# Eight token groups, a recurrence of 512 steps beside them: the second group's projections move into the third group's experts, and the recurrence serves the groups at other steps

## The reference, cut to what matters

```
k = l2norm(silu(x @ Wk)); v = silu(x @ Wv); q = silu(x @ Wq)
a = k * -sigmoid(x @ Wg);  f = sigmoid(x @ Wf1 @ Wf2)
for t in range(512):
    S = S + a[t] (x) (k[t] . S)
    S = f[t] * S
    S = S + a[t] (x) (k[t] . S) + k[t] (x) v[t]
    o[t] = q[t] . S
out = layernorm(o_placed * sigmoid(x @ Wo1 @ Wo2)) * ln_w @ Wout
```

## Time and profile before

| | us |
|---|---|
| median of 3 runs | 5178.53 |
| lowest and highest of them | 5151.21, 5182.2 |
| the profiled execution, its own time | 5154.96 |
| its span, first to last instruction | 5153.2 |
| PE, DVE, ACT, POOL busy in it | 4309.6, 3271.6, 2603.5, 1814.6 |
| mean granted clock of PE | 0.893 of full |

### The profile page before, as it was taken

The page is one execution under the profiler, slowest core; times in us unless marked ns, Lnnn a source line. Parts: engine busy times, 40 slices in busy tenths (PEclk is TensorE's granted clock), DMA queues, the critical chain, the costliest instruction groups (busy, mean ns, idle before and its releaser), DMA issues.

```text
span 5153.2 us, 114063 instructions
## 1 busy us (share of the span) xinstructions
PE 4309.6 (84%) x43126; PEld 2583.4 (50%) x43126; DVE 3271.6 (63%) x14115; ACT 2603.5 (51%) x5100; POOL 1814.6 (35%) x3734
## 2 busy tenths in 40 slices
PE   4689999999999999975699999778750079999999
PEld 4545555555555555545544446545520034446777
DVE  3187777777777777733177741699999867762111
ACT  1346777777777777751344544444430034553333
POOL 3255666666666666663132210000100023220000
PEclk9879999999999999986788989888865568998999
DMA  4500000000000000004401000010010000000000
GB/s 125 145 10 2 3 12 2 7 8 2 12 2 2 12 2 7 2 1 114 115 8 38 1 1 13 13 26 16 16 34 0 12 1 1 1 1 3 5 5 7
DMA packets 125108, 101.75 MB, mean 20 GB/s; under 512 B 22384, under 2 KB 103568, under 8 KB 124560
## 3 DMA queue, kind: packets, MB, share of 16 engines
q1 hardware_dynamic: 119952, 85.00, 6.0%
q0 software_dynamic: 4608, 9.45, 0.8%
HBM read 74.56 MB, written 19.86 MB: 18 GB/s over the span
## 4 chain that ended last, share of the span: by engine, by line
PE 58%; DVE 22%; POOL 10%; issue 4%; ACT 4%; DMA 1%; SPq 0%; POOLq 0%; DVEq 0%; ACTq 0%; PEldq 0%
PE ps L1746 6%; PE ps L1738 6%; PE ps L1357 5%; PE ps L1302 5%; PE ps L1502 4%; PE ps L1514 4%; PE ps L1278 4%; PE ps L1317 3%; PE ps L1288 3%; PE ps L1231 3%; PE ps L1543 2%; POOL arena L990 2%; POOL arena L995 2%; PE ps L1187 2%; DVE arena L2824 2%
## 5 line engine op out<-in xcount | busy, mean ns | idle before, releaser
L2294 DVE CUSTOM_DVE_ANT_0 arena<-ps,mask_win 128x256 f32<-128x256 f32 (+1 forms) x3072 | 1006.0, 386 | 156.6 <-PE ps L1302 155.7
L1910 ACT ACTIVATE arena<-ps 128x512 f32<-128x512 f32 (+1 forms) x1536 | 752.7, 544 | 490.0 <-PE ps L1317 487.5
L1317 PE MATMUL ps<-arena 32*64 32x384 f32 (+2 forms) x6144 | 703.1, 475 | 8.4 <-DVE arena L2294 7.1
L1302 PE MATMUL ps<-arena 32*64 32x192 f32 (+2 forms) x12288 | 683.6, 322 | 15.9 <-DVE arena L2294 15.4
L1746 PEld LDWEIGHTS ps<-w,arena 128*128 128x128 f32 x4096 | 544.4, 195 | 265.9 <-issue 223.0
L2174 ACT ACTIVATE arena<-ps,eb 128x512 f32<-128x512 f32 x512 | 351.7, 688 | 548.8 <-PE ps L1738 548.7
L2467 DVE CUSTOM_DVE_ANT_0 arena<-ps,mask_cau 128x512 f32<-128x512 f32 (+3 forms) x1024 | 446.6, 487 | 251.3 <-PE ps L1502 248.8
L2027 ACT ACTIVATE arena<-ps 128x512 f32<-128x512 f32 (+2 forms) x768 | 362.9, 526 | 456.2 <-PE ps L1514 456.1
L990 POOL TENSOR_SCALAR_AFFINE_SELECT arena<-arena 128x1024 f32<-128x1024 f32 x384 | 419.9, 1094 | 491.4 <-ACT arena L1910 486.1
L1746 PE MATMUL ps<-w,arena 128*128 128x128 f32 x4096 | 551.0, 278 | 26.6 <-ACT arena L2174 26.6
L1738 PE MATMUL ps<-arena,w 128*128 128x512 f32 x1024 | 534.5, 605 | 0.4
(11 more groups left out here) (348 smaller groups left out, 7572.2 us busy)
## 6 DMA issues: line engine op xcount, KB each, us to landing
w<-in_L_w_dram SPq DMA_DIRECT2D x160, 256.0 KB, 3.5
ys<-arena SPq DMA_DIRECT2D x10, 512.0 KB, 4.5
hs<-arena SPq DMA_DIRECT2D x16, 256.0 KB, 2.3
w<-in_L_w_dram SPq DMA_DIRECT2D x1, 2048.0 KB
scr_k<-arena SPq DMA_DIRECT2D x8, 256.0 KB, 2.3
scr_v<-arena SPq DMA_DIRECT2D x8, 256.0 KB, 2.9
scr_f<-arena SPq DMA_DIRECT2D x8, 256.0 KB, 3.2
arena<-scr_k SPq DMA_DIRECT2D x8, 256.0 KB, 3.5
```

The costliest lines, as they stand in the source:

```text
L1302: m = pe.matmul(ps[64 * h:64 * h + 64, bank, s.at(v) + lo:s.at(v) + hi], Q[p][r][rows, v, q0:q0 + 64], K[p][r][rows, s.k0 + lo:s.k0 + hi], ...
L1317: m = pe.matmul(out[64 * h:64 * h + 64, :, lo:hi], K[p][r][rows, t.k0 + lo:t.k0 + lo + 64], Q[p][r][rows, 0:2, t.q0 + lo:t.q0 + hi], start ...
L1910: act.activation(PTs[m % L.SLOTS][:, k * w:(k + 1) * w], bank[:, 0:w], exp, scale=-1.0)\
L2294: x = dve.tensor_tensor_reduce(out=seen, in0=bank[:, s.at(v):s.at(v) + s.kw], in1=mask, scale=1.0, scalar=NO_SCORE, op0=ALU.add, op1=ALU.m ...
```

## The change

Projections: every group but the last is now projected inside the experts of the group behind it. `normed` stands at pass 11 and `projected`/`project` at pass 15 as before for even groups, now for all, except group 1 in group 2: passes 4 and 7. The experts run through from group to group. `by_time(0)` stands at pass 13 of group 2, `by_time(1)` and `by_time(2)` at pass 27 of groups 4 and 6, `by_time(3)` at the end. Recurrence: the services stand at steps 4, 28, 64, 94 and 114 of a chunk. The first chunk's root is made by DVE itself instead of POOL. `kt_ready` counts each of the three copies, so that the squares wait for the keys' copy alone and `prepare` for all three.

```diff
+    def normed_at(self, g):
+        return 4 if g == 1 else 11
+    def projected_at(self, g):
+        return 7 if g == 1 else 15
+    def by_time_at(self, c):
+        return 13 if c == 0 else 27
...
                 if c:
-                    sp.wait_ge(R.kt_ready, c)
+                    sp.wait_ge(R.kt_ready, 3 * c)
...
-                    pool.wait_ge(R.n2_ready, c + 1)
-                    newton(pool, chain, RN, N2, T1)
-                    pool.sem_inc(R.rn_ready, 1)
+                    if c:
+                        pool.wait_ge(R.n2_ready, c)
+                        newton(pool, chain, RN, N2, T1)
+                        pool.sem_inc(R.rn_ready, 1)
...
-                        if s == 15 and beside:
+                        if use == 0 and g and s == R.projected_at(g - 1):
                             project(g - 1)
                         if s:
                             down(g, *order[s - 1])
-                        elif g and (use or beside):
+                        elif g:
                             down(g - 1, *order[-1])
...
-                    if beside:
-                        down(g, *order[-1])
-                        if S.scaled(use, g):
-                            add(g, EXPERTS - 1)
-                        project(g)
-                if use:
-                    down(S.GROUPS - 1, *order[-1])
+                g = S.GROUPS - 1
+                down(g, *order[-1])
+                if use == 0:
+                    add(g, EXPERTS - 1)
+                    project(g)
...
                     for dst, src in ((KT, KD), (FT[c % 2], FD), (VT[c % 2], VD)):
-                        m = act.activation(dst, src.rearrange("p k t -> p t k"), copy)
-                    m.then_inc(R.kt_ready, 1)
+                        act.activation(dst, src.rearrange("p k t -> p t k"), copy).then_inc(R.kt_ready, 1)
...
-                            if (e, c) == (2, 3) and beside:
+                            if use == 0 and g and at == R.normed_at(g - 1):
                                 normed(g - 1)
-                            if (e, c) == (3, 3) and beside:
+                            if use == 0 and g and at == R.projected_at(g - 1):
                                 projected(g - 1)
-                            if (e, c) == (1, 3) and use == 0 and g in (4, 6):
+                            if use == 0 and g in (2, 4, 6) and at == R.by_time_at(g // 2 - 1):
                                 by_time(g // 2 - 1)
...
                 def lengths(c):
-                    dve.wait_ge(R.kt_ready, c + 1)
+                    dve.wait_ge(R.kt_ready, 3 * c + 1)
...
-                    dve.tensor_scalar(N2, N2, 1e-24, None, ALU.max).then_inc(R.n2_ready, 1)
+                    m = dve.tensor_scalar(N2, N2, 1e-24, None, ALU.max)
+                    if c:
+                        m.then_inc(R.n2_ready, 1)
+                        return
+                    chain.link(m)
+                    newton(dve, chain, RN, N2, T1)
...
-                    dve.wait_ge(R.rn_ready, c + 1)
+                    if c:
+                        dve.wait_ge(R.rn_ready, c)
+                    dve.wait_ge(R.kt_ready, 3 * c + 3)
...
-                    if at == 28:
+                    if at == 4:
                         add_bank(0, g)
                         stats_of(g)
-                    if at == 54:
+                    if at == 28:
                         silu(g)
-                    if at == 86:
+                    if at == 64:
                         add_bank(0, g + 1)
                         stats_of(g + 1)
-                    if at == 108:
+                    if at == 94:
                         silu(g + 1)
-                    if at == 123:
+                    if at == 114:
                         lengths(c + 1)
```

More of the change, by code:

```diff
@@ L1787, in dense @@
                 for g in range(S.GROUPS):
-                    beside = use == 0 and g % 2
                     for s, (e, c) in enumerate(order):
@@ L2169, in dense @@
                 for g in range(S.GROUPS):
-                    beside = use == 0 and g % 2
                     for e in range(EXPERTS):
                         for c in range(CHUNKS):
+                            at = CHUNKS * e + c
                             act.wait_ge(S.up_done, S.result(use, g, e) * CHUNKS + c + 1)
@@ L2187, in dense @@
                                 scale(g, e - 1)
-                            if (e, c) == (0, 3) and beside and S.scaled(use, g - 1):
+                            if (e, c) == (0, 3) and g and S.scaled(use, g - 1):
                                 scale(g - 1, EXPERTS - 1)
-                    if beside:
-                        if S.scaled(use, g):
-                            scale(g, EXPERTS - 1)
-                        normed(g)
-                        projected(g)
-                        if g in (1, S.GROUPS - 1):
-                            by_time(g // 2)
+                if use == 0:
+                    g = S.GROUPS - 1
+                    scale(g, EXPERTS - 1)
+                    normed(g)
+                    projected(g)
+                    by_time(g // 2)
             attention(cau, 0, 0)
```

4 lines of the change are left out of this document (2 added, 2 removed).

## The result

The changed kernel takes 5183.41 us (median of 20 runs, 5168.01 to 5204.09); the kernel before, run beside it, 5166.34 (20 runs, 5147.94 to 5189.39). The ratio is 1.003, with a 95% interval of 1.0017 to 1.0044: slower by 17 us in the medians, 9 to 23 by the interval, which is inside the 1% that the prediction takes for no change. The prediction said 5182 and no change. Its class is right, and that the number is so close is luck: it stood on a median of three runs, 5178.53, that lies 12 us above the median of twenty, and the change cost 17 and not 3.4.

What follows compares the result with a forecast made beforehand. DVE's recurrence was taken to bound the stretch, through its start and its waits. The terms sum to +3.4 us: 5158 from the profiled 5154.96, 5182 from the median 5178.53, where the forecast was put; range 5139 to 5202.

Steps and rivals of the forecast that it cites:

- The start: Ahead of chunk 0: `prepare(0)` starts 1.9 us earlier, at 3264.9, with ACT last and Newton on DVE taking 4.0.
- Step 4: In chunk 0, DVE waits 7.6 us for group 2's bank instead of 2.94: 4.7 lost; bounds 2 and 14.
- 5.0 more: PE behind gelu 13 of group 2: `by_time(0)`, a scaling and the next gelu, partly hidden, delay the bank by 5.0 us.
- slower rival: Services come too soon for PE, which restarts at low clock after standing: +20 us, so 5199; chance 0.17.
- The rest of chunk 0: Waits of 0.7 us at steps 28 and 64, none at 94 and 114; the 1.85 before `prepare(1)` goes: +1.5 - 1.85.
- Chunk 1: Waits of 1.6 us for group 5's bank and 3.3 for keys, against 2.1 and 1.86 before: +0.9 in all.
- the same sum: Change over the whole kernel, added from start and chunks: -1.9 + 4.7 + 1.5 - 1.85 + 0.9 = +3.4 us.
- chunk 2: Last part counted: group 7's bank is early and the waits for q stay, so nothing is added.
- PE's gap: Rival: PE's 41 us gap between groups 1 and 2 is on the path, so the end comes at 5137; chance 0.04.
- Waits did come in place of the old ones: Against the rival that old waits go and none comes in the recurrence: -11.6 us, so 5167; chance 0.17.

## Why the class was right and the sum was not

**The start** held. The prediction had the copies 40.8 us behind group 1's last gelu and found them at 40.3; Newton 4.0, measured 4.05; `prepare(0)` 1.9 earlier, measured 2.2. That ACT and not the DMA would be last held too. (The signs that the prediction gives as times of a trace, as `prepare(0)` between 3260 and 3270, have to be read 24.9 us later in the trace after, by what the untouched part ahead took longer there: 3289.48 less 24.89 is 3264.6.)

**Step 4** had the right mechanism and a term too small: 7.6 us forecast, 10.1 measured, within the bounds of 2 and 14. DVE's arrival was forecast at 86.1 us of the stretch and came at 85.7. The bank was forecast at 93.7 and came at 95.8. The step that failed is "5.0 more" for the time that `by_time(0)` holds PE: from the end of gelu 13 to the bank 52.9 us were forecast and 55.5 came, 2.6 more, and gelu 13 itself ended 0.4 early. PE's timeline and two windows (busy PE first, the granted clock third from the end) show what was left out:

```profile
3282.51 1.02 PE L1750 MATMUL ps<-arena,w 128*128 128x512 f32 x2
3288.39 2.07 PE L1758 MATMUL ps<-w,arena 128*128 128x128 f32 x8 [4.85 <-ACT arena L2182]
```

```profile
3288.39:3293.37 4.98, 4.98 (x12) 3.21 (x13) 4.73 (x9) 0.52 (x1) 0.00 (x0) 0.50 0.00 0
3293.37:3336.22 42.85, 42.72 (x233) 29.63 (x232) 31.63 (x42) 23.19 (x47) 0.00 (x0) 1.00 0.00 1
```

PE stood 4.85 us as counted, and then worked 4.98 us at the 1.2 GHz level, eight downs in 2.07 instead of 1.05. At half the clock that is some 2.5 us lost, nearly all of the 2.6; the 47.9 us of before, to which the 5.0 were added, ran at a clock of 1.00 throughout:

```profile
3287.47:3335.39 47.92, 47.79 (x258) 32.94 (x257) 42.62 (x100) 25.81 (x53) 0.00 (x0) 1.00 0.00 1
```

The prediction had this in its slower rival and in its upper bound, but not in the forecast.

**The rest of chunk 0** held nearly to the row: bank to bank 77.1 forecast, 77.13 measured; 0.7 and 0.7 against 0.69 and 0.86. **Chunk 1** too: 1.6 and 3.3 against 1.23 and 2.96, and PE's stand at pass 9 of group 5 was 30.14 for "some 29". With the measured waits the same sum is -2.2 + 7.2 + 1.55 - 1.85 + 0.24 = +4.9; the stretch grew by 5.7, and the remaining 0.8 shows in no wait.

**The step that failed most** is not in the sum at all. After chunk 2 the prediction says "Nothing" and adds up, as if the code behind the recurrence cost the same whenever it starts. It cost 10.5 us more in the traces, nearly twice what the stretch lost, with PE at a lower clock for the same matmuls; why the clock was lower is not settled.

**The rivals.** PE's gap was worth nothing: it closed, and the end came later. Waits did come in place of the old ones. The slow restart was seen, behind the copies and behind the stand in chunk 1 (2.04 us for the bias row, 2.08 for eight downs), yet cost some 2.5 us in chunk 0 and none that shows in chunk 1, not 20; its price assumed that four restarts fall where nothing hides them. The Trainium skill, ScalarE: Activation LUTs, section "What ACT_TABLE_LOAD costs", would have a switch of tables take 2.66 us with its drain. The trace does not agree: the row says 1.28 and the next gelu stands 0.01 behind it, and the start came out by the row.

**What the change did, in one pair of numbers.** The projections' move brought the bank of group 2 24.1 us earlier (from 119.9 to 95.8 us of the stretch); the services' move (29) and the earlier start (2.2) made DVE ask for it 31.2 earlier (117.0 to 85.7). The difference, 7.1, is the loss at step 4. Asking eight steps later there, with all of chunk 0's later services and three of chunk 1's set 2 to 10 steps later as well, turned the stretch's loss of 5.7 into a gain of 10.5.

## What to carry to other kernels

When a producer and the point that asks for its result are moved together, work out both new times before anything else: the difference of the two shifts is added to the wait, and a consumer that had no slack and is moved further than its producer pays it in full. Split single profiles by stage before comparing them: here 25 of 41 us were chance in untouched code, and changes there from one execution to the next hide a gain of 10 us. And when a stretch ends earlier or later, look at what starts at a low clock behind it as well: in these traces that part differed by as much as the largest wait of the stretch, with the same instructions.

## What the hardware showed that was not expected

Code that no edit touched can change its length by more than an edit saves. In single traces, some 1.5 us of added work ahead of the causal attention went with a part 5.9 us shorter in the changed kernel (589.2 against 595.1), and 3.4 us in the kernel before with one 13.7 longer (598.3 against 584.6); the medians neither confirm nor exclude the second. The lengths of the unchanged part, counted from PE's first matmul, were not spread evenly: they gathered at 573, 576 to 577 and 584.5 to 585 us over fourteen executions.

PE at half clock shows in the rows of single passes (eight downs in 2.07 us against 1.05) after a stand as short as 4.85 us, and also after one of 30.14:

```profile
3532.29 2.04 PE L1728 MATMUL ps<-eb,arena 8*128 8x128 f32 x8 [30.14 <-DVE X L2738]
3534.26 2.08 PE L1758 MATMUL ps<-w,arena 128*128 128x128 f32 x8
```

The length of the stand did not change what eight downs cost then (2.07 and 2.08), but the clock came back after 4.98 us of work in one case and 6.84 in the other. At half the clock that is some 2.5 and 3.4 us lost, where the prediction's slower rival took a longer stand to cost no more than a short one.
